# x read in 32-wide blocks and turned by VectorE, in another order of work: two graph attention layers in float32 on one Trainium2 core

## The chip, the cores and the metric

The kernel runs on one core of a Trainium2 chip. Its engines are named as in the profile: PE is TensorE (PEld its weight loads), DVE is VectorE, ACT is ScalarE, POOL is GpSimd, SP is SyncE, which here only issues DMAs. The metric is the time on the device in microseconds, lower is better.

## What is computed

128 graphs, each with 128 nodes of 384 features. Two layers follow each other; each is an attention over 12 heads of width 32 in which the adjacency matrix is added to the scores, then a residual and a layer norm.

```python
# x: (128, 128, 384), adj: (128, 128, 128)
def L0(x, adj):                        # scale = 384 ** -0.5
    q, k, v = x @ Wq.T, x @ Wk.T, x @ Wv.T + bv        # split into 12 heads
    scores = einsum('bqhd,bkhd->bhqk', q, k) * scale + 2 * adj
    p = softmax(where(any(scores != 0), scores, -inf)) # a row of zeros gives 0
    return einsum('bhqk,bkhd->bqhd', p, v) @ Wo.T + bo
def L1(x, adj):                        # scale = 32 ** -0.5
    q, k, v = x @ Wq + bq, x @ Wk + bk, x @ Wv + bv
    scores = einsum(q, k) * scale + beta * adj
    return einsum(softmax(where(adj > 0, scores, -9e15)), v)
x = layernorm(x + L0(x, adj))
x = layernorm(x + L1(x, adj))
```

## The kernel before

**Pairs and stages.** The graphs are worked on two at a time, in 64 pairs. One run of each engine's `body` is an iteration n; it does different stages of different pairs: `n` is the pair whose layer 0 scores are made now, `p1` the next one, `m1` to `m5` are one to five pairs back. In a name such as `attend(1, m3, 0, r)` the first number is the layer, then come the pair and the graph of the pair. Iterations -1 to 7 and the last ones are written out; 54 between them run in a loop of two iterations a turn. Each engine's `body` is a hand-written list, and an engine works through it strictly in that order. The engines meet only through semaphores.

**Products.** A projection is a float32 product made of three faster ones: both factors are split into a high part and a rest (`_hi`, `_lo`), and `split_product` (L363) adds hi*hi, lo*hi and hi*lo over three chunks of 128 features: nine matmuls. They are 256 columns wide for q and k (`project_qk`, six a layer and pair) and 384 for v and the output (`project_v`, `project_out0`).

**x before the first projection.** SP loads a graph of x to `x_in` (node on the partition, `load_x`). PE transposes it in three blocks (`transpose_x`, L348), ACT takes the high part from PSUM (`high_xT`, L514), DVE the rest (`low_xT`, L714). POOL adds the output bias to `x_in` and keeps it as `x_bo` for the residual (L873).

**Layer 0's softmax.** `scores` (PE, L416) writes four banks. `negate` (DVE, L692) adds the adjacency, negates, and finds the row minimum. ACT makes the exps (L589). `fold_scores0` (POOL, L896 and L899) adds the negated scores in halves, and `abs_max` (DVE, L741) finishes that, to know rows of zeros; `inverse_sums0` (DVE, L776, L780) gives the factor and `normalise0` (POOL, L914, three pieces) applies it. `flip_probs` (DVE, L708) transposes each 32 by 32 block of the probabilities into `flip0`, and `spread_probs` (SP, L300) moves the blocks to their places in `prob0T` by four DMAs of 192 KB. `attend` (PE, L432) uses them. `flip0` is also where the fold writes, so `fold_scores0` waits until the spread of the graph before has landed. Layer 1 does the same without the fold, through `stage` and `prob1T`.

**PSUM.** Eight banks: four for scores, four as a ring for all else; the list `RING_USERS` deals the ring's banks out in turn, and a PE block first waits for the last reader of its bank.

**Narrow blocks.** Scores use 32 rows of the array and attention 32 columns at a time, in 12 matmuls each, and transposes are plain float32 matmuls against the identity. All other blocks are the projections' 128 by 128 products.

Of the kernel before, what the change touches and what calls it, by code (L numbers as in the profile page):

```python
# [31 lines left out]
NB = N // HD  # L32
PAIRS = NG // 2
# [9 lines left out]
FIRST, LAST = -1, PAIRS + 4  # L43
# [10 lines left out]
RING_USERS = ["pv0_0", "pv1_0", "g1_0", "ot_0", "v1_0", "wo_0", "v0_1", "xt0",  # L54
              "xt1", "g1_1", "pv1_1", "v1_1", "ot_1", "g1_2", "pv0_1", "g0_0",
              "g0_1", "g1_3", "wo_1", "g1_4", "g1_5", "g0_2", "x1t0", "g0_3",
              "g0_4", "g0_5", "x1t1", "v0_0"]
RING = 4
assert len(RING_USERS) % RING == 0
# [52 lines left out]
def build(nc, x, adj, wts, bv0, bo0, bq1, bk1, bv1, beta, out):  # L112

    with ExitStack() as ctx:
# [26 lines left out]
        x_in = [sb(f"x_in{b}", [P, 2, D]) for b in range(2)]  # L141
# [9 lines left out]

        xT_hi, xT_lo = sb("xT_hi", [P, C, G2], F32R), sb("xT_lo", [P, C, G2], F32R)
# [33 lines left out]
        x_loaded, adj0_loaded, adj1_loaded = sems("x_loaded"), sems("adj0_loaded"), sem("adj1_loaded")  # L186
# [8 lines left out]
        xt_done, x1t_done = sem("xt_done"), sem("x1t_done")  # L195
# [34 lines left out]
        def _(sp):  # L230
            def load_x(q):
                if q.valid():
                    b = q.parity

                    sp.wait_ge(xt_done, q.plus(-2).count(1, 1, 1))
                    sp.wait_ge(x_bo_done, q.plus(-2).count(1, 1, 1))
                    for g in range(2):
                        sp.dma_start(x_in[b][:, g, :], x[bass.ds(2 * q.index() + g, 1)].rearrange("g (j a) d -> a j (g d)", j=NB)
                                     ).then_inc(x_loaded[b], 16)
# [41 lines left out]
            load_weights(WV0)  # L281
# [21 lines left out]
            def body(r, off):  # L303
# [3 lines left out]
                spread_probs(1, m4, 1)  # L307
                keep_x1(m3)
                if not is_peeled(r, off, -1):
                    load_adj0(p1)  # L310
                spread_probs(0, m1, 1)
                store(m5, 1)
                spread_probs(1, m3, 0)
                load_adj1(m1)
                spread_probs(0, n, 0)
                load_x(p2)
                store(m4, 0)
# [8 lines left out]
        def _(pe):  # L326

            read = [(xt_lo_done, 0, 0, 0, 0)] * 4
# [132 lines left out]
            def body(r, off):  # L461
# [5 lines left out]
                transpose_out1(m4, 0, r)  # L467
                project_v(1, m2, 0, r)
                project_out0(m1, 0, r)
                project_v(0, n, 1, r)  # L470
                scores(1, m3, 1, r)
                transpose_x(p1, 0, r)
                transpose_x(p1, 1, r)
                project_qk(1, m2, 1, r)
                attend(1, m4, 1, r)
                project_v(1, m2, 1, r)
                transpose_out1(m4, 1, r)
                project_qk(1, m2, 2, r)
# [492 lines left out]
```

## Time and profile before

| | us |
|---|---|
| median of 3 runs | 2143.37 (2141.89 to 2144.39) |
| the profiled execution | 2141.5 |
| its span, first to last instruction | 2139.7 |
| PE busy in the span | 2061.3 |
| DVE, ACT, POOL busy | 1870.9, 1834.0, 1511.2 |

The span is what the trace covers; the time of an execution has 1.8 us around it. A busy time counts overlapping instructions of an engine once. PE is pipelined: a row of it lasts until its result is out, so rows overlap, and how long PE is held is read from one start to the next. SP's rows show the issue of DMAs, not their transfer.

### The profile page before, as it was taken

How to read it: one execution, taken by the hardware profiler on the slowest of the kernel's cores; microseconds unless marked ns; L12 is line 12 of the kernel's file. 1: busy time of each engine (PE TensorE's matmuls, PEld its weight loads, DVE VectorE, ACT ScalarE, POOL GpSimd, SP SyncE). 2: the span in 40 equal slices, each digit the busy share in tenths (PEclk: the TensorE clock that was granted, in tenths of full speed). 3: DMA queues.
4: the chain of work that ended last, by engine and by line, in shares of the span. 5: the costliest groups of instructions: out<-in, count | busy, mean ns of one | idle time of the engine just before them, and what ended most of it. 6: DMA issues, size and time to landing. Idle time of an engine off the chain costs nothing.

```text
span 2139.7 us, 86405 instructions
## 1 busy us (share of the span) xinstructions
PE 2061.3 (96%) x23808; PEld 1924.5 (90%) x23808; DVE 1870.9 (87%) x8452; ACT 1834.0 (86%) x7688; POOL 1511.2 (71%) x2059
## 2 busy tenths in 40 slices
PE   5799999999999999999999999999999999999984
PEld 4799999999999999999999999999999999999873
DVE  4588989999999999999999999999999899999875
ACT  4489888889889889889889889888988988988875
POOL 3667777777777777777777777777777777777663
PEclk9999999999999999999999999999999999999997
DMA  4255665665565565565565565556556556556454
GB/s 133 60 131 132 149 160 126 147 157 131 146 155 132 145 155 134 145 150 136 143 150 139 144 146 142 141 146 148 135 146 152 131 146 155 131 144 158 119 136 119
DMA packets 234654, 299.36 MB, mean 140 GB/s; under 512 B 26704, under 2 KB 226384, under 8 KB 234576
## 3 DMA queue, kind: packets, MB, share of 16 engines
q1 hardware_dynamic: 234576, 298.43, 56.5%
q8 instruction: 36, 0.59, 0.1%
q14 instruction: 42, 0.34, 0.0%
HBM read 46.67 MB, written 25.17 MB: 34 GB/s over the span
## 4 chain that ended last, share of the span: by engine, by line
PE 86%; POOL 5%; issue 3%; DMA 3%; DVE 2%; SPq 2%; ACT 0%; POOLq 0%; DVEq 0%
PE r_bank L365 22%; PE r_bank L366 20%; PE r_bank L367 20%; PE s_bank L416 10%; PE r_bank L432 8%; PE r_bank L348 2%; DMA prob0T<-flip 2%; PE r_bank L358 2%; PE r_bank L444 2%; POOL prob L914 2%; SPq L300 1%; POOL flip L896 1%; DVE flip L708 1%; DMA prob1T<-stage 0%; POOL norm L857 0%
## 5 line engine op out<-in xcount | busy, mean ns | idle before, releaser
L589 ACT ACTIVATE prob<-neg_s,heads 128x128 f32<-128x128 f32 x3072 | 1190.1, 393 | 49.5 <-DVE flip L708 42.5
L589 ACT ACTIVATION_READ_ACCUMULATOR prob<-neg_s,heads 128x1 f32 x3072 | 592.1, 193 | 0.0
L896 POOL TENSOR_TENSOR flip<-neg_s 128x768 f32<-128x768 f32 x128 | 235.7, 1842 | 265.3 <-DMA prob0T<-flip 255.1
L914 POOL TENSOR_TENSOR prob<-prob,heads 128x512 f32<-128x512 f32 x384 | 388.8, 1040 | 19.2 <-DVE heads L780 15.5
L365 PE MATMUL r_bank<-xT_hi,w_hi 128*128 128x256 f32 x1152 | 344.6, 299 | 16.6 <-DVE xT_lo L714 10.9
L692 DVE CUSTOM_DVE_ANT_0 neg_s<-s_bank,bias 128x128 f32<-128x128 f32 x1536 | 333.9, 286 | 15.4 <-PE s_bank L416 14.3
L365 PE MATMUL r_bank<-x1T_hi,w_hi 128*128 128x256 f32 x1152 | 342.3, 297 | 3.3 <-DVE x1T_lo L714 1.8
L692 DVE CUSTOM_DVE_ANT_0 neg_s<-s_bank,adj 128x128 f32<-128x128 f32 x1536 | 334.0, 286 | 1.7 <-PE s_bank L416 0.5
L366 PE MATMUL r_bank<-xT_lo,w_hi 128*128 128x256 f32 x1152 | 326.0, 283 | 0.0
L367 PE MATMUL r_bank<-xT_hi,w_lo 128*128 128x256 f32 x1152 | 325.9, 283 | 0.0
L367 PE MATMUL r_bank<-x1T_hi,w_lo 128*128 128x256 f32 x1152 | 323.9, 281 | 0.0
L366 PE MATMUL r_bank<-x1T_lo,w_hi 128*128 128x256 f32 x1152 | 323.8, 281 | 0.0
L692 DVE DVE_READ_ACCUMULATOR2_ANT heads<- 128x1 f32 x3072 | 256.1, 83 | 0.1
L708 DVE STREAM_TRANSPOSE flip<-prob 128x1536 f32<-128x1536 f32 x128 | 227.7, 1779 | 24.3 <-POOL prob L914 18.9
L365 PEld LDWEIGHTS r_bank<-xT_hi,w_hi 128*128 128x128 f32 x1152 | 218.2, 189 | 32.6 <-DVE xT_lo L714 11.4
L365 PEld LDWEIGHTS r_bank<-x1T_hi,w_hi 128*128 128x128 f32 x1152 | 217.2, 189 | 12.4 <-DVE x1T_lo L714 2.0
L708 DVE STREAM_TRANSPOSE stage<-prob 128x1536 f32<-128x1536 f32 x128 | 224.0, 1750 | 3.8 <-DMA prob1T<-stage 3.8
L366 PEld LDWEIGHTS r_bank<-xT_lo,w_hi 128*128 128x128 f32 x1152 | 219.0, 190 | 0.0
L367 PEld LDWEIGHTS r_bank<-xT_hi,w_lo 128*128 128x128 f32 x1152 | 218.4, 190 | 0.0
L366 PEld LDWEIGHTS r_bank<-x1T_lo,w_hi 128*128 128x128 f32 x1152 | 217.7, 189 | 0.0
L367 PEld LDWEIGHTS r_bank<-x1T_hi,w_lo 128*128 128x128 f32 x1152 | 217.0, 188 | 0.0
L854 POOL TENSOR_SCALAR norm<-norm 128x1 f32<-128x1 f32 x256 | 56.7, 221 | 177.1 <-DVE norm L673 161.6
(83 smaller groups left out, 5443.9 us busy)
## 6 DMA issues: line engine op xcount, KB each, us to landing
prob0T<-flip SPq DMA_DIRECT2D x512, 192.0 KB, 3.6
prob1T<-stage SPq DMA_DIRECT2D x512, 192.0 KB, 3.6
x_in<-in_x_dram SPq DMA_DIRECT2D x128, 192.0 KB, 3.2
x_late<-x SPq DMA_DIRECT2D x64, 384.0 KB, 4.3
out_dram<-y SPq DMA_DIRECT2D x128, 192.0 KB, 2.7
adj<-in_adj_dram SPq DMA_DIRECT2D x256, 64.0 KB, 2.9
prob<-in_L_gnn_Wq_dram SPq DMA_DIRECT2D x1, 576.0 KB, 5.7
prob0T<-in_L_gnn_Wk_dram SPq DMA_DIRECT2D x1, 576.0 KB, 6.6
```

Source lines behind the costliest of these rows:

```text
L348: mm = pe.transpose(ring(f"xt{g}")[:, c * P:(c + 1) * P], x_in[q.parity][:, g, c * P:(c + 1) * P], ident[:])
L365: pe.matmul(dst, a_hi(c), b_hi(c), start=(c == 0), stop=False)
L366: pe.matmul(dst, a_hi(c), b_lo(c), start=False, stop=False)
L367: mm = pe.matmul(dst, a_lo(c), b_hi(c), start=False, stop=(c == C - 1))
L416: mm = pe.matmul(s_bank[j][:, c * N:(c + 1) * N], qT[layer][q.parity][rows, c, m], kT[layer][q.parity][rows, c, m], start=True, stop=True)
L432: mm = pe.matmul(ring(name)[HD * j:HD * (j + 1), c * N:(c + 1) * N], v[layer][q.parity][:, g, f], probT[layer][:, :, HC * c + j, :], start ...
L589: act.activation(prob[layer][:, h, :], neg_s[layer][:, h, :], ACT.Exp, bias=neg_max[layer][:, h:h + 1], scale=-1.0, accum_out=row_sum[laye ...
L692: dve.tensor_tensor_reduce(neg_s[layer][:, h, :], s_bank[b][:, (h // HC) * N:(h // HC + 1) * N], (adj0, bias1)[layer][q.parity][:, g, :], ...
L708: dve.transpose(flip[layer].rearrange("p (j h b) -> p h j b", j=NB, h=H), prob[layer][:].rearrange("p h (j a) -> p h j a", j=NB)).then_inc ...
L854: pool.tensor_scalar(var_eps[layer][g][:], mean_var[layer][g][:, 1:2], EPS, None, ALU.add).then_inc(rstd_steps[layer], 1)
L896: pool.tensor_tensor(fold_a, neg_s[0][:, :, 0:N // 2], neg_s[0][:, :, N // 2:N], ALU.add).then_inc(fold_steps, 1)
L914: pool.tensor_tensor(prob[0][:, hs, :], prob[0][:, hs, :], inv_sum0[:, hs].unsqueeze(2).to_broadcast([P, HC, N]), ALU.mult).then_inc(probn ...
```

## The change

Where x is turned: SP now loads x a second time, as `x_q`. Four DMAs a pair (`load_q`) put the 96-feature column block i of both graphs on partitions 32i to 32i+31, with the row block of 32 nodes along the free dimension. One 32 by 32 block transpose of DVE a graph (`flip_x`) then gives `xT` in SBUF, with the features in another order of rows; the rows of the three layer 0 weights are loaded in that same order (`load_rows`, four DMAs each, two of the weights from ACT's queue). `transpose_x` and its two places in the ring are gone. ACT takes the high part from `xT`, POOL the rest (`low_xT`, before on DVE). `x_bo` is loaded directly and POOL adds the bias in place.

The order of all five lists is another one, and so is `RING_USERS`. The second graph's values are projected one iteration earlier, and there is one more written-out iteration at the start.

```diff
-FIRST, LAST = -1, PAIRS + 4
+FIRST, LAST = -2, PAIRS + 4
...
+            def load_q(q):
+                if q.valid():
+                    sp.wait_ge(xflip_done, q.count(1, 0, 0))
+                    for i in range(NB):
+                        sp.dma_start(x_q[HD * i:HD * (i + 1), :, :],
+                                     x[bass.ds(2 * q.index(), 2)].rearrange("g (j a) d -> a (g j) d", j=NB)[:, :, QD * i:QD * (i + 1)]
+                                     ).then_inc(xq_loaded, 16)
...
-            load_x(Pair(0, 0))
-            load_weights(WQ0)
-            load_weights(WK0)
+            load_q(Pair(0, 0))
+            load_rows(WV0)
...
-            def transpose_x(q, g, r):
-                if q.valid():
-                    pe.wait_ge(*last_read(read, BANK[f"xt{g}"], r))
-                    read[BANK[f"xt{g}"]] = (xt_lo_done, q.off, 1, g, 1)
-                    pe.wait_ge(x_loaded[q.parity], q.loads(2))
-                    for c in range(C):
-                        mm = pe.transpose(ring(f"xt{g}")[:, c * P:(c + 1) * P],
-                                          x_in[q.parity][:, g, c * P:(c + 1) * P], ident[:])
-                    mm.then_inc(xt_done, 1)
...
+            def flip_x(q, g):
+                if q.valid():
+                    dve.wait_ge(xq_loaded, q.count(8 * NB, 1, 8 * NB))
+                    dve.wait_ge(xt_lo_done, q.plus(-1).count(1, g, 1))
+                    dve.transpose(xT[:, :, g * N:(g + 1) * N].rearrange("p c (j a) -> p c j a", j=NB),
+                                  x_q[:, g * NB:(g + 1) * NB, :].rearrange("p j (c b) -> p c j b", c=C)
+                                  ).then_inc(xflip_done, 1)
...
+            def low_xT(q, g):
+                if q.valid():
+                    pool.wait_ge(xt_hi_done, q.count(1, g, 1))
+                    if g == 0:
+                        pool.wait_ge(v_done[0], q.count(1, 0, 0))
+                        pool.wait_ge(g_done[0], q.count(3, 0, 0))
+                    m = slice(g * N, (g + 1) * N)
+                    pool.tensor_tensor(*(t.rearrange("p c (a j) -> p c a j", j=NB) if i != 1 else t.rearrange("p c (j a) -> p c a j", j=NB)
+                                        for i, t in enumerate((xT_lo[:, :, m], xT[:, :, m], xT_hi[:, :, m].bitcast(F32)))), ALU.subtract
+                                      ).then_inc(xt_lo_done, 1)
```

On PE, in the middle of an iteration, before: layer 1's scores are followed by the transposes of x, and its attention stands alone between projections.

```order
L416 MATMUL s_bank<-k1T,q1T 128x128 x12
L348 MATMUL r_bank<-ident,x_in 128x128 x6
L365 MATMUL r_bank<-x1T_hi,w_hi 128x256
L366 MATMUL r_bank<-x1T_lo,w_hi 128x256
L367 MATMUL r_bank<-x1T_hi,w_lo 128x256
...
L432 MATMUL r_bank<-prob1T,v_0 32x128 x12
L365 MATMUL r_bank<-w_hi,x1T_hi 128x384
```

The same place now: the transposes of x are gone, and the attention of layer 0's first graph, that of layer 1's second and the scores of layer 1 stand next to each other.

```order
L368 MATMUL r_bank<-w_hi,x1T_lo 128x384
L433 MATMUL r_bank<-prob0T,v_0 32x128 x12
L433 MATMUL r_bank<-prob1T,v_1 32x128 x12
L417 MATMUL s_bank<-k1T,q1T 128x128 x12
L366 MATMUL r_bank<-w_hi,o0T_hi 128x384
```

Over a whole iteration the runs of narrow blocks (scores, attentions, transposes that touch each other) go from nine to six.

On POOL, from `normalise0` of the second graph to the next fold, before:

```order
L914 TENSOR_TENSOR prob<-prob,heads 128x512 x3
L884 TENSOR_SCALAR mask<-adj 128x128
L886 TENSOR_SCALAR adj<-adj,beta_col 128x128
L889 TENSOR_TENSOR bias_1<-adj,mask 128x128
...
L906 TENSOR_TENSOR y_0<-y_0,x_late 128x384
L873 TENSOR_TENSOR x_bo<-x_in,bo_row 128x384 x2
L896 TENSOR_TENSOR flip<-neg_s 128x768
```

and now, from the last step of the first bias on:

```order
L897 TENSOR_TENSOR bias_0<-adj,mask 128x128
L906 TENSOR_TENSOR xT_lo<-xT,xT_hi 128x3x128
L892 TENSOR_SCALAR mask<-adj 128x128
L894 TENSOR_SCALAR adj<-adj,beta_col 128x128
L897 TENSOR_TENSOR bias_0<-adj,mask 128x128
L863 TENSOR_SCALAR norm_0<-norm_0 128x1
L866 TENSOR_TENSOR norm_0<-norm_0,neg_half 128x1
L870 TENSOR_SCALAR norm_0<-norm_0 128x1
L906 TENSOR_TENSOR xT_lo<-xT,xT_hi 128x3x128
L915 TENSOR_TENSOR flip<-neg_s 128x768
```

The residuals of both layers moved behind the fold; both `low_xT` and one `inverse_std` stand ahead of it.

On SP, the DMAs around the border of two iterations, before:

```order
L300 DMA prob0T<-flip 128x1x384 x4
...
L238 DMA x_in<-in_x_dram 128x1x384
...
L259 DMA out_dram<-y_0 32x4x384
L300 DMA prob1T<-stage 128x1x384 x4
...
L269 DMA x_late<-x_0 128x768
...
L246 DMA adj_0<-in_adj_dram 128x1x128
...
L300 DMA prob0T<-flip 128x1x384 x4
```

and now:

```order
L309 DMA prob1T<-stage 128x1x384 x4
...
L236 DMA x_q<-in_x_dram 32x8x96
...
L275 DMA x_late<-x_0 128x768
...
L309 DMA prob0T<-flip 128x1x384 x4
```

The four issues of `x_q` (one is shown) stand between those of `prob1T` and those of `prob0T`. The loads of `x_bo` and both adjacency loads are now ahead of these `prob1T`.

## Rows read from the trace of the kernel before

**Rows 1.** The page: busy time, share of the span, instructions of each engine

```profile
PE 2061.3 (96%) x23808; PEld 1924.5 (90%) x23808; DVE 1870.9 (87%) x8452; ACT 1834.0 (86%) x7688; POOL 1511.2 (71%) x2059
```

**Rows 2.** Busy time by stretch: length, PE, PEld, DVE, ACT, POOL, clock, DMA share, GB/s

```profile
130.00:2045.00 1915.00, 1912.33 (x22296) 1791.14 (x22292) 1740.74 (x7910) 1705.07 (x7189) 1403.84 (x1914) 1.00 0.58 143
```

**Rows 3.** Timeline of PE: start, length, line, out<-in, count

```profile
98.56 0.95 PE L416 MATMUL s_bank<-k0T,q0T 32*128 32x128 f32 x24
...
1007.35 0.86 PE L432 MATMUL r_bank<-prob0T,v 128*32 128x128 f32 x24
1008.03 0.84 PE L432 MATMUL r_bank<-prob1T,v 128*32 128x128 f32 x24
...
1016.87 0.88 PE L348 MATMUL r_bank<-ident,x_in 128*128 128x128 f32 x6
1017.51 0.37 PE L365 MATMUL r_bank<-x1T_hi,w_hi 128*128 128x256 f32 x1
1017.71 0.28 PE L366 MATMUL r_bank<-x1T_lo,w_hi 128*128 128x256 f32 x1
1017.83 0.28 PE L367 MATMUL r_bank<-x1T_hi,w_lo 128*128 128x256 f32 x1
...
1018.75 0.86 PE L432 MATMUL r_bank<-prob1T,v 128*32 128x128 f32 x24
1019.54 0.44 PE L365 MATMUL r_bank<-w_hi,x1T_hi 128*128 128x384 f32 x1
...
2045.54 0.95 PE L416 MATMUL s_bank<-k0T,q0T 32*128 32x128 f32 x24
```

**Rows 4.** Timelines of POOL, DVE and SP: the ring from fold to fold

```profile
1021.08 1.85 POOL L896 TENSOR_TENSOR flip<-neg_s 128x768 f32<-128x768 f32 x1 [1.22 <-DMA prob0T<-flip]
...
1024.04 0.55 DVE L741 TENSOR_REDUCE heads<-flip 128x12 f32<-128x384 f32 x1 [0.43 <-POOL flip L899]
...
1025.41 3.04 POOL L914 TENSOR_TENSOR prob<-prob,heads 128x512 f32<-128x512 f32 x3
...
1028.57 1.78 DVE L708 STREAM_TRANSPOSE flip<-prob 128x1536 f32<-128x1536 f32 x1 [0.27 <-POOL prob L914]
...
1030.38 3.02 SPq L300 DMA_DIRECT2D prob0T<-flip  x4
...
1036.73 1.84 POOL L896 TENSOR_TENSOR flip<-neg_s 128x768 f32<-128x768 f32 x1 [2.58 <-DMA prob0T<-flip]
```

**Rows 5.** The same timelines, in the turn before

```profile
1004.87 1.84 POOL L896 TENSOR_TENSOR flip<-neg_s 128x768 f32<-128x768 f32 x1 [2.26 <-DMA prob0T<-flip]
...
1008.14 0.54 DVE L741 TENSOR_REDUCE heads<-flip 128x12 f32<-128x384 f32 x1
...
1013.04 1.69 SPq L246 DMA_DIRECT2D adj<-in_adj_dram  x2
1014.83 3.05 SPq L300 DMA_DIRECT2D prob0T<-flip  x4
```

**Rows 6.** Waits of the whole span: total us, times, longest

```profile
POOL flip L896 <- DMA prob0T<-flip: 255.1, 127, 8.3
...
DVE heads L741 <- POOL flip L899: 43.5, 71, 4.4
```

**Rows 7.** Timeline of POOL: from the first make_bias1 to what follows the second

```profile
1012.70 0.66 POOL L884 TENSOR_SCALAR mask<-adj 128x128 f32<-128x128 f32 x1
...
1016.91 1.01 POOL L906 TENSOR_TENSOR y<-y,x_late 128x384 f32<-128x384 f32 x1
```

**Rows 8.** Groups by shape (busy us, mean ns), and the page's DMA queue

```profile
L714 DVE TENSOR_TENSOR xT_lo<-r_bank,xT_hi 128x384 fp32r<-128x384 f32 x128 | 63.1, 532 | 6.9 <-ACT xT_hi L514 4.1 <-issue 2.8
...
q1 hardware_dynamic: 234576, 298.43, 56.5%
```

**Rows 9.** Timelines of PE and POOL at the start

```profile
15.74 0.55 PE L365 MATMUL r_bank<-xT_hi,w_hi 128*128 128x256 f32 x1 [9.71 <-DVE xT_lo L714]
...
16.17 0.25 POOL L939 TENSOR_SCALAR bq1s<-bqk 128x3 f32<-128x3 f32 x1 [14.51 <-DMA bqk<-in_L_gnn_bk_dram]
```

More of the change, by code:

```diff
@@ L32 @@
 NB = N // HD
+QD = D // NB
 PAIRS = NG // 2
@@ L139, in build @@
         neg_half = sb("neg_half", [P, 1])
-        x_in = [sb(f"x_in{b}", [P, 2, D]) for b in range(2)]
+        x_q = sb("x_q", [P, 2 * NB, QD])
         x_bo = [sb(f"x_bo{b}", [P, 2, D]) for b in range(2)]
@@ L313, in body @@
                 spread_probs(1, m3, 0)
+                spread_probs(0, n, 0)
+                store(m4, 0)
                 load_adj1(m1)
-                spread_probs(0, n, 0)
-                load_x(p2)
-                store(m4, 0)
+                load_x(p1)
+                if not is_peeled(r, off, -1):
+                    load_adj0(p1)
+                spread_probs(1, m3, 1)
             iterations(sp, body)
@@ L326, in _ @@
         def _(pe):
-            read = [(xt_lo_done, 0, 0, 0, 0)] * 4
+            read = [(v_out[0], 0, 0, 0, 0)] * 4
             s_read = [(neg_done[0], 0, 0, 0, 0)] * HC
@@ L502, in _, with load_rows, rows_xT @@
         def _(act):
+            def load_rows(i):
+                for k in range(NB):
+                    act.dma_start(w_stage[i][HD * k:HD * (k + 1), :, :],
+                                  wts[i][QD * k:QD * (k + 1), :].rearrange("(c b) o -> b c o", c=C)).then_inc(w_loaded[i], 16)
+            load_rows(WQ0)
+            load_rows(WK0)
             def high_weights(*which):
                 for i in which:
-                    act.wait_ge(w_loaded[i], 16)
+                    act.wait_ge(w_loaded[i], 16 * (NB if i in (WV0, WQ0, WK0) else 1))
                     act.activation(w_hi[i][:], w_stage[i], ACT.Copy).then_inc(w_hi_done[i], 1)
+            def rows_xT(g):
+                return xT[:, :, g * N:(g + 1) * N].rearrange("p c (j a) -> p c a j", j=NB)
             def high_xT(q, g):
                 if q.valid():
-                    act.wait_ge(xt_done, q.count(1, g, 1))
+                    act.wait_ge(xflip_done, q.count(1, g, 1))
                     if g == 0:
@@ L513, in high_xT @@
                         act.wait_ge(g_done[0], q.count(3, 0, 0))
[L514 to L516 removed]
+                    act.activation(xT_hi[:, :, g * N:(g + 1) * N].rearrange("p c (a j) -> p c a j", j=NB), rows_xT(g), ACT.Copy).then_inc(xt_hi_done, 1)
             def high_x1T(q, g):
@@ L595, in body @@
                 n = Pair(r, off)
-                m5, m4, m3, m2, m1, p1 = (n.plus(-5), n.plus(-4), n.plus(-3), n.plus(-2), n.plus(-1), n.plus(1))
-                high_o0T(m1, 0)
-                exps(1, m3, 0, 2, 4)
-                out1T_out(m4, 0)
-                exps(1, m3, 0, 4, 8)
-                qk_out(1, m2, 0, r)
-                exps(1, m3, 0, 8, 12)
-                norm_apply1(m5, 1)
-                exps(0, n, 0, 0, 6)
-                high_xT(p1, 0)
+                m4, m3, m2, m1, p1 = (n.plus(-4), n.plus(-3), n.plus(-2), n.plus(-1), n.plus(1))
+                exps(1, m3, 0, 0, 6)
+                high_xT(p1, 0)
+                exps(1, m3, 0, 6, 10)
+                qk_out(1, m2, 0, r)
+                qk_out(1, m2, 1, r)
+                high_o0T(m1, 0)
+                exps(1, m3, 0, 10, 12)
                 high_xT(p1, 1)
@@ L870, in residual0 @@
                     pool.wait_ge(x_loaded[b], q.loads(2))
-                    pool.wait_ge(y0_done, q.plus(-2).count(1, 1, 1))
                     for g in range(2):
-                        pool.tensor_tensor(x_bo[b][:, g, :], x_in[b][:, g, :], bo_row[:], ALU.add
+                        pool.tensor_tensor(x_bo[b][:, g, :], x_bo[b][:, g, :], bo_row[:], ALU.add
                                            ).then_inc(x_bo_done, 1)
@@ L919, in body @@
                 n = Pair(r, off)
-                m4, m2, m1 = (n.plus(-4), n.plus(-2), n.plus(-1))
+                m4, m3, m2, m1, p1 = (n.plus(-4), n.plus(-3), n.plus(-2), n.plus(-1), n.plus(1))
                 normalise0(m1, 1)
                 make_bias1(m2, 0)
+                low_xT(p1, 0)
                 make_bias1(m2, 1)
-                residual1(m4, 0)
-                residual0(n, r)
+                inverse_std(1, m4, 0)
+                low_xT(p1, 1)
                 fold_scores0(n, 0)
@@ L930, in body @@
                 residual1(m4, 1)
-                inverse_std(1, m4, 0)
+                residual0(n, r)
+                inverse_std(1, m4, 1)
                 inverse_std(0, m1, 1)
                 fold_scores0(n, 1)
-                inverse_std(1, m4, 1)
+                residual1(m3, 0)
                 if is_peeled(r, off, 0):
```

132 lines of the change are left out of this document (62 added, 70 removed).

## The prediction

> **What bounds the kernel now.** I read the page's busy line, then two stretches by engine, then the tensor engine's timeline, then the waits, and last I followed the one loop of dependences that the waits point to.
>
> Busy shares leave little room: PE 96%, DVE 87%, ACT 86% [rows 1]. Between 130 and 2045 us PE is busy 1912.33 of 1915 us at a granted clock of 1.00, that is the 2.4 GHz level, against 1741 us of DVE, 1705 of ACT and 1404 of POOL [rows 2]. What comes after 2045 is the drain. The scores of layer 0's second graph start at 98.56 us for pair 2 and at 2045.54 us for pair 63 [rows 3]: 61 pairs in 1946.98 us, **31.92 us a pair**. So PE sets the pace, and what is taken from it is won, until something else comes due.
>
> That something is visible. POOL's fold waits for the landing of `prob0T` 127 times, 255 us in all [rows 6]. The fold writes `flip0`, the very buffer that the turned probabilities of the graph before leave by DMA. So there is a **ring**: fold, abs_max and inverse (DVE), normalise0 (POOL), flip (DVE), four DMAs issued by SP, landing, next fold. It runs once a graph, twice a pair. One turn of it starts at 1021.08 and ends at 1036.73: 15.65 us, made of 2.96 (fold, until DVE takes over at 1024.04), 1.37 to the start of normalise0, 3.04 of that, 0.12, a 1.78 transpose, 0.03, and 6.35 from SP's first issue to the next fold [rows 4]. Nothing in it stands idle. The other turn of a pair must take 31.92 - 15.65 = 16.27 us. The one from 1004.87 shows what it has to spare: its fold of 2.96 us would be over at 1007.8 and DVE comes at 1008.14; its transpose, in the same rhythm, ends at about 1014.5 and SP comes at 1014.83, after other loads [rows 5]. That is 0.3 twice. The ring alone therefore needs about 15.65 + 15.7 = **31.35 us a pair**, only 0.57 under today's pace. In 71 of 128 folds DVE already stood waiting for POOL [rows 6], which says the same.
>
> **The change, part by part.**
>
> *PE loses work.* The six transposes of x take 1016.87 to 1017.51, 0.64 us a pair [rows 3]. The order also joins narrow blocks. Two neighbouring attentions start 0.68 apart (1007.35, 1008.03), one alone holds PE for 0.79 (1018.75 to 1019.54), and the projection's first matmul behind a narrow block is followed 0.20 later (1017.51 to 1017.71) where 0.12 is the rhythm (1017.71 to 1017.83; the rows are longer and overlap) [rows 3]. So a run of narrow blocks pays about 0.1 on its way in and as much on its way out. Before, a pair has nine such runs (of transposes, scores, attentions), after it six. Three fewer at somewhat under 0.1 a side come to about 0.23. PE's need falls to 31.92 - 0.64 - 0.23 = **31.05 us**.
>
> *DVE is even.* It drops two `xT_lo` subtractions of 532 ns [rows 8] and gains two transposes 384 wide. A transpose 1536 wide takes 1.78 [rows 4]; a quarter of that is 0.44, and at most it keeps a fixed part of some 0.2, 0.6. Two of them cost -0.2 to +0.15 us a pair. I take 0. DVE is busy 1741/60 = 29.0 us a pair and stays below both other bounds.
>
> *ACT is even.* `high_xT` reads SBUF instead of PSUM, same width; nothing between -0.1 and +0.4 a pair reaches the path with 28.4 busy of 31.
>
> *POOL takes over `low_xT`*, two subtractions 384 wide, both in the stretch between normalise0 of one turn and the fold of the next. Nearest row: 1.01 us for a plain add of that width [rows 7]. The stretch is from 1028.45 (1025.41 + 3.04) to 1036.73: 8.28 us [rows 4]. In it now stand two `make_bias1`, 4.21 us (1012.70 to 1016.91) [rows 7], one `inverse_std` (it fits in the 1.4 between fold and normalise0 [rows 4]) and the two subtractions, 2.0, with 0.1 of gaps: 7.7 us. Spare: 0.6. So each may cost 1.3 before the fold is late. `low_xT` reads `xT` in steps of 128 bytes, which no row shows; I bound it by 1.0 and 2.0 and take 1.0 to 1.3.
>
> The Trainium skill (GPSIMD Engine Reference, § 7 Performance pitfalls for Q7 kernels) says that a read whose step is over 8 bytes costs a GpSimd kernel half as much again. No run here shows it. By that estimate, 1.5 each, the fold would be 0.4 late.
>
> *SP issues four more DMAs a pair*, `x_q`, 29 instead of 25. Four of `prob0T` hold it for 3.02 us [rows 4], 0.76 each, so SP is busy some 22 us of 31. The order matters: from the issue for the first graph's probabilities, 15 DMAs (4 `prob0T`, the store, 2 `adj1`, 2 `x_bo`, 2 `adj0`, 4 `prob1T`), then the four `x_q`, then `keep_x1`, and only then the second turn's `prob0T`. That is 15 x 0.76 + 4q + 0.6 = 12.0 + 4q, and it must be over within the ring's 15.7. It is, with q up to 0.93. With q = 0.76 there are 0.7 us to spare. Bounds for q: 0.76 from that row, and twice that, 1.5, since one has 256 pieces where one of `prob0T` has 128; less than 0.76 would change nothing. I take 0.76, as the time of an issue is not seen to follow its size: four `prob0T` of 192 KB take 3.05, two loads of `adj`, 64 KB each, 1.69 [rows 5].
>
> *DMA engines.* The hardware queue's 234576 packets fill 56.5% of 16 engines [rows 8], 0.082 us each. `x_q` adds 1024 a pair, 65536: at the same time each +15.7 points, at half of it +8. The share goes to 65 to 72%. Landings in the ring may lengthen: 0 to 0.3 a turn; `x_q` is in flight just ahead of one turn in two. I take 0.1 a pair.
>
> *The start is longer.* PE's projections begin at 15.74, on `xT_lo` from DVE; POOL's first real step waits until 16.17 for the last small load [rows 9]. Now `xT_lo` is POOL's, behind that load, and three more DMAs are issued ahead of it (17 instead of 14): 16.2 + 3 x 0.76 = 18.5, plus two `low_xT` of 1.0 to 1.4, so PE begins at 20.5 to 21.3, some 5.2 later. Also the second graph's values are projected ahead of the first scores: nine matmuls 384 wide at 1.5 times the 0.12 of a 256 wide one [rows 3], 1.6 us. The scores, and with them the ring, start **6.8 us** later (4 to 8). Nothing hides this: from there on the ring decides.
>
> *The drain* keeps its chain (last scores, exps, flip, spread, attend, layer norm, store): 0, within 2 us.
>
> **The sum.** PE would allow 31.05, the ring 31.35, DVE less; with 0.1 for landings and jitter now that nothing else absorbs them, 31.45 us a pair. 60 pairs x (31.92 - 31.45) = 28.2 us won, 6.8 lost: the span goes from 2139.7 to 2118.3. The profiled execution took 2141.5, 1.8 over its span, and the median of the runs shown is 1.9 above that: **2122.0 us**. With 31.3 to 31.7 a pair and a start of 4 to 8 us it is 2110 to 2138.
>
> **The rivals.**
>
> *PE keeps the pace.* The ring's turns may shrink, as SP and DVE now come to them in another order, and landings vary. Then a pair takes PE's 31.05 to 31.15: 60 x 0.82 = 49 less, 6.8 more, 2101 us. For it: PE is the busiest engine on every view. Against: no link of the turn in [rows 4] is touched by the change.
>
> *The gain is swallowed on POOL.* With `low_xT` at 1.5 each, by the row's width and a cost half as large again, the fold is 0.4 late in one turn a pair: 31.85, 60 x 0.07 = 4 won, 6.8 lost, 2146 us, the same as before. This is the time that the rule of the GPSIMD Engine Reference in the Trainium skill gives. [...]
>
> *SP is late, the kernel slower.* If one `x_q` takes SP q over 0.93, the second turn's `prob0T` issue waits and each turn of that kind grows by 4(q - 0.93). At q = 1.2 that is 1.1 us a pair: 31.45 + 1.1 = 32.55, 60 x 0.63 = 38 more, plus 6.8: 2188 us. By over 0.2% slower it is from q = 1.04. For it: twice the pieces in each DMA. Against: the even pace named above.
>
> **How the numbers follow.** Chances: forecast 0.50, PE's pace 0.22, swallowed on POOL 0.12, SP late 0.12, the rest, mostly a longer start, 0.04. The time is the forecast's, 2122. The range leaves out the slow rival and the fastest edge: 2101 to 2143. About 0.2%, 4.3 us, is what a measurement of this kernel can tell. Faster than 2139.1: the forecast, PE's pace and a part of the swallowed case, 0.76. Same: 0.11. Slower: 0.13.
>
> **What would show it.** The fold on POOL should still wait for `prob0T`, and now PE should show small idle times, 0.2 to 0.4 a pair, in front of transposes or first attentions. If PE is gapless the second case holds. A `low_xT` row above 1.3 and folds that start without waiting show the third; SP's first `prob0T` issue coming more than 0.1 behind its transpose in one turn of two shows the fourth. The first projection should start near 20 us. I am wrong altogether if the narrow blocks do not save PE anything, or if attentions placed early wait for probabilities.

## The result: slower, 2157.3 us, with PE no longer the bound

The changed kernel takes 2157.29 us (median of 4 runs, 2155.69 to 2157.82) beside 2143.08 for the kernel before on the same chip: a ratio of 1.0065, 95% interval 1.0053 to 1.0077. The forecast was 2122 us, with a range of 2101 to 2143. The profiled execution's span went from 2139.7 to 2153.9 us, 14.2 more. The forecast was faster, and the time moved the other way. The page of the changed kernel, busy time of each engine (before: [rows 1]):

```profile
PE 2011.7 (93%) x23424; PEld 1871.0 (87%) x23424; DVE 1872.6 (87%) x8452; ACT 1871.8 (87%) x7688; POOL 1662.0 (77%) x2187
```

PE is 50 us less busy, as intended, and the kernel is longer. Its stretch in the middle by engine (length, PE, PEld, DVE, ACT, POOL, clock, DMA share, GB/s; before: [rows 2]):

```profile
600.00:1600.00 1000.00, 973.53 (x11505) 908.20 (x11506) 912.96 (x4151) 911.18 (x3764) 809.21 (x1063) 1.00 0.63 157
```

PE now stands idle 26.5 us of 1000, at a granted clock of 1.00 as before, that is at 2.4 GHz. I take the length of a pair from the first `normalise0` of pair 8 and of pair 60: 31.91 us before, 31.89 after. PE is busy 0.9735 x 31.89 = 31.05 us of a pair, the number of the prediction to the hundredth; only the time does not follow it. (A busy time is a rough measure of a need, since short waits can hide in overlapping rows: the runs below with this same list on PE give 31.04 to 31.31.) The waits of the whole span (total us, times, longest) say who holds it (before: [rows 6]):

```profile
POOL flip L915 <- DMA prob0T<-flip: 191.6, 125, 6.1
...
ACT prob L597 <- DVE flip L716: 80.6, 64, 3.4
DVE heads L750 <- POOL flip L918: 61.9, 102, 8.2
PE r_bank L433 <- DVE v L778: 58.4, 61, 12.2
...
POOL prob L933 <- DVE heads L789: 42.9, 65, 1.9
```

The fold still waits for the spread 125 times, DVE waits for the fold in 102 turns instead of 71, and PE waits once a pair, at its first attention, for values that DVE has not yet taken out. The page's chain of work that ended last was PE's before and no longer is (shares of the span, before and after):

```profile
PE 86%; POOL 5%; issue 3%; DMA 3%; DVE 2%; SPq 2%; ACT 0%; POOLq 0%; DVEq 0%
...
POOL 39%; issue 30%; DVE 11%; PE 10%; DMA 4%; SPq 2%; POOLq 2%; DVEq 1%; ACT 0%; ACTq 0%
```

Two turns of the ring, one pair, on the timelines of POOL, DVE and SP (before: [rows 4] and [rows 5]):

```profile
1032.65 1.84 POOL L915 TENSOR_TENSOR flip<-neg_s 128x768 f32<-128x768 f32 x1 [0.24 <-DMA prob0T<-flip]
...
1036.97 3.04 POOL L933 TENSOR_TENSOR prob<-prob,heads 128x512 f32<-128x512 f32 x3
...
1040.13 1.78 DVE L716 STREAM_TRANSPOSE flip<-prob 128x1536 f32<-128x1536 f32 x1 [0.23 <-POOL prob L933]
...
1041.94 3.02 SPq L309 DMA_DIRECT2D prob0T<-flip  x4
1045.18 0.62 SPq L265 DMA_DIRECT2D out_dram<-y  x1
...
1048.45 1.85 POOL L915 TENSOR_TENSOR flip<-neg_s 128x768 f32<-128x768 f32 x1 [2.25 <-DMA prob0T<-flip]
...
1051.43 0.55 DVE L750 TENSOR_REDUCE heads<-flip 128x12 f32<-128x384 f32 x1
...
1053.12 3.04 POOL L933 TENSOR_TENSOR prob<-prob,heads 128x512 f32<-128x512 f32 x3 [0.51 <-DVE heads L789]
...
1055.94 0.55 DVE L778 TENSOR_TENSOR v<-r_bank,bv_row 128x384 f32<-128x384 f32 x1
1056.41 1.77 DVE L716 STREAM_TRANSPOSE flip<-prob 128x1536 f32<-128x1536 f32 x1
...
1056.41 0.53 SPq L275 DMA_DIRECT2D x_late<-x  x1
1058.21 3.02 SPq L309 DMA_DIRECT2D prob0T<-flip  x4
...
1064.57 1.84 POOL L915 TENSOR_TENSOR flip<-neg_s 128x768 f32<-128x768 f32 x1 [0.39 <-DMA prob0T<-flip]
```

15.80 and 16.12 us: 31.92. SP's first issue comes 0.03 behind each transpose, so SP is not late; POOL is through with its other work 0.24 and 0.39 us before each of the folds that follow `low_xT`, so POOL is not late either. I measured every link over turns 10 to 117, 54 of each graph (means, us; "g0" is the turn that starts with the first graph's fold; "landing" is from the issue of the fourth DMA until it has landed):

| link | before g0 | before g1 | after g0 | after g1 |
|---|---|---|---|---|
| fold on POOL | 2.92 | 2.94 | 2.92 | 2.93 |
| until abs_max starts | 0.03 | **0.27** | 0.03 | 0.03 |
| abs_max to the factor | 1.22 | 1.46 | 1.22 | 1.52 |
| gap, normalise0 | 3.20 | 3.13 | 3.18 | 3.12 |
| gap, flip | 1.90 | 1.90 | 1.90 | **1.98** |
| until SP issues | 0.03 | **0.23** | 0.03 | 0.03 |
| first to fourth issue | 2.02 | 2.04 | 1.98 | 2.04 |
| landing of the fourth | 4.18 | 4.32 | **4.51** | **4.38** |
| landing to next fold | 0.08 | 0.07 | 0.08 | 0.07 |
| turn | 15.57 | 16.35 | 15.83 | 16.10 |

Before, only 0.23 + 0.21 = 0.44 us of a pair were slack (the bold entries of "before g1", less the 0.03 that these links take at least), so the ring needed 31.47. After, that slack is gone and the links that carry load grew by 0.33 (landing g0), 0.06 (landing g1), 0.06 (factor) and 0.08 (the values that DVE takes between `negate` and the flip, seen at 1055.94), together 0.53; three others shrank by 0.07 in all. The ring's pace is 31.93, and the kernel's. It is a coincidence of sizes that this is also what PE needed before.

Where the 14.2 us came in, by the first `normalise0` of a pair, after minus before:

| pair 0 | pair 8 | pair 20 | pair 60 | pair 63 | end of span |
|---|---|---|---|---|---|
| +8.24 | +11.73 | +12.63 | +10.82 | +13.52 | +14.19 |

So the start costs 8.2, the first eight pairs 3.5, the long middle gives back 0.9, the last three pairs cost 2.7, and the drain 0.7. Timelines of POOL and PE at the start: the first scores of the kernel before, then the changed kernel (before: [rows 9]):

```profile
25.68 0.95 PE L416 MATMUL s_bank<-k0T,q0T 32*128 32x128 f32 x24
...
17.13 0.25 POOL L960 TENSOR_SCALAR bq1s<-bqk 128x3 f32<-128x3 f32 x1 [15.47 <-DMA bqk<-in_L_gnn_bk_dram]
18.23 2.32 POOL L906 TENSOR_TENSOR xT_lo<-xT,xT_hi 128x384 fp32r<-128x384 f32 x2 [0.84 <-ACT xT_hi L524]
...
20.81 0.55 PE L366 MATMUL r_bank<-xT_hi,w_hi 128*128 128x256 f32 x1 [20.81 <-POOL xT_lo L906]
...
32.69 0.95 PE L417 MATMUL s_bank<-k0T,q0T 32*128 32x128 f32 x24
...
35.59 2.32 POOL L906 TENSOR_TENSOR xT_lo<-xT,xT_hi 128x384 fp32r<-128x384 f32 x2 [15.04 <-ACT xT_hi L524]
37.88 1.82 POOL L915 TENSOR_TENSOR flip<-neg_s 128x768 f32<-128x768 f32 x1
```

PE begins at 20.81 (forecast 20.5 to 21.3) and the first scores come 7.0 us later than before (forecast 6.8). Then the first fold finds both `low_xT` of pair 1 ahead of it on POOL, and the ring starts 8.2 late. The groups of the changed kernel by shape (busy us, mean ns) and its DMA queue price the new operations (before: [rows 8]):

```profile
L906 POOL TENSOR_TENSOR xT_lo<-xT,xT_hi 128x384 fp32r<-128x384 f32 x128 | 156.3, 1222 | 15.9 <-ACT xT_hi L524 15.9
L524 ACT ACTIVATE xT_hi<-xT 128x384 fp32r<-128x384 f32 x128 | 115.2, 901 | 2.1 <-DVE xT L729 2.1
L729 DVE STREAM_TRANSPOSE xT<-x_q 128x384 f32<-128x384 f32 x128 | 71.9, 563 | 5.6 <-DMA x_q<-in_x_dram 5.6
...
q1 hardware_dynamic: 303456, 322.43, 60.3%
```

### The profile page after: what moved, and what is told of

The parts are those of the page before. It is cut to its first block, busy times and chain, and to the rows that moved or that the text cites. A ratio compares the mean times of both kernels' runs of the same rounds, so it can differ in the third digit from the quotient of the medians.

```text
span 2153.9 us, 86362 instructions
## 1 busy us (share of the span) xinstructions
PE 2011.7 (93%) x23424; PEld 1871.0 (87%) x23424; DVE 1872.6 (87%) x8452; ACT 1871.8 (87%) x7688; POOL 1662.0 (77%) x2187
## 3 DMA queue, kind: packets, MB, share of 16 engines
q1 hardware_dynamic: 303456, 322.43, 60.3%
## 4 chain that ended last, share of the span: by engine, by line
POOL 39%; issue 30%; DVE 11%; PE 10%; DMA 4%; SPq 2%; POOLq 2%; DVEq 1%; ACT 0%; ACTq 0%
POOL prob L933 11%; POOL flip L915 9%; POOL norm L866 4%; DMA prob0T<-flip 4%; DVE flip L716 4%; POOL adj L894 3%; POOL xT_lo L906 3%; POOL mask L892 3%; PE r_bank L366 3%; PE r_bank L368 2%; PE r_bank L367 2%; DVE norm L678 2%; SPq L309 2%; DVE neg_s L700 2%; POOL norm L863 2%
## 5 line engine op out<-in xcount | busy, mean ns | idle before, releaser
L366 PE MATMUL r_bank<-x1T_hi,w_hi 128*128 128x256 f32 x1152 | 332.6, 289 | 5.0 <-DVE x1T_lo L722 5.0
L716 DVE STREAM_TRANSPOSE flip<-prob 128x1536 f32<-128x1536 f32 x128 | 227.0, 1773 | 21.4 <-POOL prob L933 21.3
L906 POOL TENSOR_TENSOR xT_lo<-xT,xT_hi 128x384 fp32r<-128x384 f32 x128 | 156.3, 1222 | 15.9 <-ACT xT_hi L524 15.9
```

Source lines behind the costliest of these rows:

```text
L366: pe.matmul(dst, a_hi(c), b_hi(c), start=(c == 0), stop=False)
L716: dve.transpose(flip[layer].rearrange("p (j h b) -> p h j b", j=NB, h=H), prob[layer][:].rearrange("p h (j a) -> p h j a", j=NB)).then_inc ...
L906: pool.tensor_tensor(*(t.rearrange("p c (a j) -> p c a j", j=NB) if i != 1 else t.rearrange("p c (j a) -> p c a j", j=NB) for i, t in enum ...
```

## The experiments

My theory: the ring through `flip0` sets the pace, and the changed order made it longer, above all by what SP issues behind the first graph's `prob0T`. Rivals: the traffic of `x_q` slows the landings; or the order has another bound of its own; or the new path of x costs what it saves. "Pair" below is the mean of pairs 8 to 60. Each kernel was timed beside the one before on the same chip, and its ratio is to that time, which was 2142.3 to 2143.6 us.

| kernel | median us | ratio to before, 95% | pair | PE busy in 600:1600 |
|---|---|---|---|---|
| before | 2143.08 | | 31.91 | 1000.00 |
| after | 2157.29 | 1.0065 (1.0053 to 1.0077) | 31.89 | 973.53 |
| own_after | 2130.75 | 0.9939 (0.9923 to 0.9954) | 31.67 | 980.12 |
| own_before | 2131.42 | 0.9940 (0.9925 to 0.9956) | 31.89 | 1000.00 |
| sp_order | 2148.72 | 1.0025 (1.0016 to 1.0034) | 31.74 | 978.44 |
| store_first | 2147.61 | 1.0028 (1.0019 to 1.0038) | 31.70 | 979.56 |
| xq_once | 2157.91 | 1.0060 (1.0046 to 1.0074) | 31.92 | 973.18 |
| low_plain | 2158.57, one run | | 31.92 | 974.21 |
| own_after_v | 2127.03 | 0.9934 (0.9917 to 0.9951) | 31.64 | 989.67 |
| best1 | 2117.33 | 0.9876 (0.9860 to 0.9893) | 31.52 | 988.80 |
| x_only | 2436.38 | 1.1374 (1.1355 to 1.1393) | 36.64 | 956.24 |
| x_only_own | 2382.39 | 1.1114 (1.1096 to 1.1133) | 35.94 | 954.72 |
| x_only2 | 2139.42 | 0.9982 (0.9973 to 0.9992) | 31.68 | 993.71 |
| x_only2_own | 2109.67 | 0.9844 (0.9827 to 0.9860) | 31.38 | 999.51 |

### Is it the ring? Cut it in both kernels

The fold writes a free part of `stage` instead of `flip0`, and so needs no landing. The same edit in both kernels:

```diff
-        fold_a = flip0[:, 0:H * N // 2].rearrange("p (h k) -> p h k", h=H)
-        fold_b = flip0[:, H * N // 2:H * N * 3 // 4].rearrange("p (h k) -> p h k", h=H)
+        fold_a = stage[:, H * N:H * N * 3 // 2].rearrange("p (h k) -> p h k", h=H)
+        fold_b = fold_a[:, :, 0:N // 4]
...
-                    pool.wait_ge(probT_loaded[0], q.count(16 * NB, g, 0))
```

> The changed kernel, but the fold of layer 0 writes to a free part of `stage` instead of to `flip0`, so it no longer waits for the spread of the graph before to land. Theory R (ring: fold, abs_max, normalise0, flip, spread, landing, fold sets the pace of 31.9 us a pair now): the ring is cut, a pair falls to about PE's 31.05 to 31.3, 60 pairs x 0.7 = 40 us less, some 2115 us. Rival E (the engines' new orders collide elsewhere, DVE and ACT waits; the ring only looks tight): a pair stays at 31.7 to 31.9, within 10 us of 2157.

> The kernel before with the same cut of the ring. Theory R says that PE, not the ring, set the pace before (PE busy 1912 of 1915 us): the middle stays at 31.9 us a pair, and only the first pairs, where PE is not full, get shorter: 5 to 25 us less, 2118 to 2138. If the ring had set the pace before as well, a pair would get shorter in the middle too.

The changed kernel falls by 26.5 us, the kernel before by 12. In the kernel before nothing changes in the middle (31.89, PE 1000.00 of 1000): it wins while the pipeline fills, where PE is not yet full and the ring decides, 258 us for the first eight pairs before and 248 with the cut. In the changed kernel 14 of its gain lie in those pairs too (261 and 247), and the rest in the middle. So the ring was the bound in the changed kernel, shown. But the 40 us that I expected did not come: a pair falls only to 31.67, far from PE's 31.05, so there is a second bound close below. The waits of own_after between 600 and 1600 us:

```profile
PE r_bank L433 <- DVE v L778: 14.8, 31, 0.5
```

### What lengthened the landing?

sp_order: both `adj` loads and the store are issued ahead of the first graph's `prob0T`, only `load_x` behind.

```diff
-                spread_probs(0, n, 0)
-                store(m4, 0)
                 load_adj1(m1)
-                load_x(p1)
                 if not is_peeled(r, off, -1):
                     load_adj0(p1)
+                store(m4, 0)
+                spread_probs(0, n, 0)
+                load_x(p1)
```

> The changed kernel with another order on SP only: both adjacency loads and the store of m4 are issued ahead of layer 0's first spread of the iteration instead of right behind it. Theory S (the store and the loads that start right behind the spread lengthen the landing of its fourth DMA, 4.18 us before, 4.51 now): it falls back to about 4.2, a pair gets 0.3 shorter, 18 us less, 2139 us. Theory X (the added traffic of x_q does it): no change, 2157 within 4.

store_first: the store alone is moved ahead, the loads stay behind.

```diff
+                store(m4, 0)
                 spread_probs(0, n, 0)
-                store(m4, 0)
                 load_adj1(m1)
```

> The changed kernel with one move alone: SP issues the store of layer 1's rows ahead of the DMAs of prob0T for the first graph, so that it is no longer the DMA right behind them; the loads of adj1 and x_bo stay behind. My theory: it is the write to device memory right behind that makes the landing of the fourth DMA 0.3 us longer: 4.51 falls to 4.2, that turn of the ring from 15.83 to 15.55, and the time by 60 x 0.25 = 15 us at most, less what the order's other loops hold: 2142 to 2152 us. Rival: any DMA 3 us behind does it, loads too: the landing stays at 4.4 to 4.5 and the time at 2155 to 2158 us.

xq_once: `x_q` is loaded for pair 0 only, so all layer 0 projections use pair 0's rows of x, and 252 DMAs are left out.

```diff
             def load_q(q):
-                if q.valid():
+                if is_peeled(q.r, q.off, 0):
...
-                    dve.wait_ge(xq_loaded, q.count(8 * NB, 1, 8 * NB))
+                    dve.wait_ge(xq_loaded, 16 * NB)
```

> The changed kernel, but x_q is loaded for pair 0 only and all pairs turn that x: four DMAs a pair, 1024 small packets, are left out (the result is that of other inputs). Theory X (traffic and issues of x_q lengthen the ring): the landings fall back to 4.2, 0.3 to 0.4 a pair less, 2135 us. Theory S: landings stay, 2155 to 2158 us.

Landing of the fourth DMA and length of the turns, means over the same turns:

| | landing g0 | landing g1 | turn g0 | turn g1 |
|---|---|---|---|---|
| after | 4.51 | 4.38 | 15.83 | 16.10 |
| sp_order | 4.19 | 4.39 | 15.57 | 16.18 |
| store_first | 4.01 | 4.37 | 15.37 | 16.34 |
| xq_once | 4.49 | 4.42 | 15.83 | 16.11 |
| x_only2 (below) | 3.94 | 4.37 | 15.32 | 16.37 |

One first-graph turn of store_first on the timelines of SP and POOL, with two loads where the changed kernel has the store:

```profile
1006.44 3.02 SPq L309 DMA_DIRECT2D prob0T<-flip  x4
1009.76 1.41 SPq L259 DMA_DIRECT2D adj<-in_adj_dram  x2
...
1012.43 1.83 POOL L915 TENSOR_TENSOR flip<-neg_s 128x768 f32<-128x768 f32 x1 [1.71 <-DMA prob0T<-flip]
```

The store is the cause: without it right behind, two loads of `adj` (64 KB each) in its place, the landing is 0.50 shorter, more than I had claimed. Loads behind do less: in x_only2, further below, nothing at all is issued for 3.9 us behind the fourth DMA, and it lands after 3.94; the two loads of `adj` make it 4.01, and two loads of x (192 KB each), in sp_order and in the kernel before, 4.19 and 4.18. So in the kernel before the store was not next: a load of x was, and the store came 4.45 us behind the fourth DMA, when that had landed. `x_q` does nothing. The store is behind the second graph's DMAs in every kernel here, and that landing is 4.3 to 4.4 everywhere. What the store does to the DMA ahead of it, these runs don't show. The time followed only in part: sp_order won 9 of the 18 us expected of it, store_first 10 of at most 15. In store_first the ring got 0.46 shorter in one turn and the pair only 0.19: turn g1 grew from 16.10 to 16.34, since `abs_max` now comes 0.18 behind the fold and the factor takes 1.63 instead of 1.52. There DVE is late; I take it for the second bound that own_after met, which no run here isolates.

### The price of `low_xT`

low_plain reads `xT` without its 128-byte steps, so `xT_lo` pairs values that don't belong together.

```diff
-                    pool.tensor_tensor(*(t.rearrange("p c (a j) -> p c a j", j=NB) if i != 1 else t.rearrange("p c (j a) -> p c a j", j=NB)
+                    pool.tensor_tensor(*(t
```

> The changed kernel, but low_xT on POOL reads and writes its three operands in plain order instead of reading xT in steps of 128 bytes (the rests then stand in the wrong places). If the step costs, low_xT falls from 1222 ns to the 1010 of a plain subtraction; if POOL shares a port with DVE at that place and the step is free, it stays at 1200. In either case the ring has no part in it, and the time stays at 2157 within 5.

Its group:

```profile
L906 POOL TENSOR_TENSOR xT_lo<-xT,xT_hi 128x384 fp32r<-128x384 f32 x128 | 129.4, 1012 | 16.4 <-ACT xT_hi L524 16.4
```

1012 ns plain, 1222 with the step: 21% more, inside the 1.0 to 1.3 that I took. The Trainium skill (GPSIMD Engine Reference, § 7 Performance pitfalls for Q7 kernels) gives half as much again for such a step; for this subtraction of two inputs, one of them with the step, the measurement decides, 21%. And the kernel is no faster for it (2158.57, a single run), so the rival on POOL falls.

### The bounds behind the ring

own_after_v: own_after, and DVE takes the second graph's values out ahead of the long `negate`.

```diff
-                negate(0, n, 0, (0, 1, 2, 3))
                 values_out(0, n, 1)
+                negate(0, n, 0, (0, 1, 2, 3))
```

> The changed kernel with the ring cut (fold in `stage`), and on DVE the second graph's values, values_out(0, n, 1), taken out of PSUM ahead of negate(0, n, 0) instead of behind it. With the cut alone a pair takes a steady 31.67 us with PE idle 0.5 in front of the first attention. Theory V: that is a second loop, PE's scores (1, m2, 0), DVE's negates, values_out, the bank that the attention needs; moved ahead, the wait goes and a pair comes to PE's 31.05 to 31.2: 60 x 0.5 = 30 us less, some 2101 us. Rival D: DVE as a whole (busy 29.1 and many short waits) is what takes 31.67; then nothing or at most 5 us is won.

PE's wait at the first attention is gone, but a pair takes 31.64 instead of 31.67, where I had expected at most 31.2 and 2101 us. The next loop stood right behind. One pair of own_after_v, timelines of PE, its weight loads, DVE and POOL:

```profile
994.97 0.95 PE L417 MATMUL s_bank<-k1T,q1T 32*128 32x128 f32 x24
...
996.10 0.29 DVE L700 CUSTOM_DVE_ANT_0 neg_s<-s_bank,bias 128x128 f32<-128x128 f32 x1 [0.88 <-PE s_bank L417]
...
999.57 0.54 DVE L750 TENSOR_REDUCE heads<-stage 128x12 f32<-128x384 f32 x1
...
1001.28 3.04 POOL L932 TENSOR_TENSOR prob<-prob,heads 128x512 f32<-128x512 f32 x3 [0.55 <-DVE heads L789]
...
1011.17 1.24 POOL L906 TENSOR_TENSOR xT_lo<-xT,xT_hi 128x384 fp32r<-128x384 f32 x1
...
1012.46 0.19 PEld L366 LDWEIGHTS r_bank<-xT_hi,w_hi 128*128 128x128 f32 x1 [0.43 <-POOL xT_lo L906]
...
1026.62 0.95 PE L417 MATMUL s_bank<-k1T,q1T 32*128 32x128 f32 x24
```

From layer 1's scores (994.97) DVE negates, then finds the zero rows of the second graph (999.57); POOL normalises it, makes both biases, a layer norm's factor and the second `low_xT` (done at 1012.41); PE starts the next pair's projection at once (1012.46), after a wait, and comes to the same scores of the next pair at 1026.62: 31.65 us, in which POOL, PE and DVE each had to wait for the step before. This loop exists only because `low_xT` now is POOL's and stands behind `normalise0`; before, PE's transposes and DVE fed that projection.

best1: own_after_v, with the second `low_xT` directly behind the first.

```diff
                 low_xT(p1, 0)
+                low_xT(p1, 1)
                 make_bias1(m2, 1)
                 inverse_std(1, m4, 0)
-                low_xT(p1, 1)
```

> The changed kernel with the fold and the turned probabilities in buffers of their own, values_out ahead of negate, and both low_xT ahead of the second make_bias1 and of inverse_std on POOL. My theory: once the ring is cut, what holds a pair at 31.65 us is the loop from layer 1's scores over negate, normalise0 and low_xT back to the projection; with low_xT 3 us earlier PE's wait for it goes, and PE's own need is the bound: 31.1 to 31.3 us a pair, 2098 to 2110 us, and PE busy over 98% of its middle. Rival: the loops of the order lie close together, the next one (the bias or the layer norm's factor, now later) holds 31.5 or more, 2118 us or more.

9.7 us faster than own_after_v, and the wait for `xT_lo` has left the middle, so that loop was a bound. But a pair still takes 31.52, and I had expected 31.1 to 31.3 and at most 2110 us, so the rival came nearer. Waits of PE between 600 and 1600 us in best1:

```profile
PE r_bank L359 <- ACT x L576: 5.0, 32, 0.2
PE r_bank L433 <- DMA prob1T<-stage: 4.4, 15, 0.5
```

These are 9 of its 11 idle us; half of them are now at an attention of layer 1, which waits for the landing of its own probabilities. Which loop lies behind that I did not settle.

### The new path of x without the new order

These four keep the lists of the kernel before and add only the new path of x; where its steps stand is my choice (`residual0` moves behind the first `normalise0` with it). x_only puts each `low_xT` ahead of a `make_bias1`, both `flip_x` together, `load_q` behind the first spread; x_only_own adds the cut.

```diff
                 normalise0(m1, 1)
+                low_xT(p1, 0)
                 make_bias1(m2, 0)
+                low_xT(p1, 1)
                 make_bias1(m2, 1)
```

> The kernel before in its own order, with only the new way of x: x_q, flip_x on DVE where low_xT stood, low_xT on POOL ahead of both make_bias1, residual0 behind normalise0; x_q is loaded one pair earlier. No transposes on PE, so PE needs 31.92 - 0.64 = 31.28 us a pair. Theory R: the ring, with the store behind the second turn only, needs 31.47, so 60 x 0.4 = 24 less, 5 more at the start: 2124 us. If the new order of work and not the ring's length were what kept the changed kernel at 31.93, it would be PE's pace: 2110 us. If the way of x itself costs (POOL late with the fold), 2143 or more.

> The same with the fold in `stage`: the ring cut. Theory R: PE's pace, 31.28 us a pair, and shorter first pairs: 2131 (the kernel before with the cut) + 5 - 60 x 0.6 = 2100 us. Rival: as in the changed kernel, another loop holds at 31.6 or more: 2120 us.

Both are over a tenth slower, and both theories missed, for a reason that the waits of x_only name:

```profile
POOL xT_lo L906 <- ACT xT_hi L524: 354.8, 64, 15.4
DVE xT L729 <- POOL xT_lo L906: 234.4, 124, 3.7
```

ACT makes `xT_hi` late in its list, where it stood when PE made the transposes. `low_xT` early on POOL waits 5.5 us a pair for it, with the biases and the fold queued behind. PE then stands idle 44 us between 600 and 1600, and its granted clock there is 0.93 (0.96 in x_only_own) where every other kernel here has 1.00; what the clock adds was not separated. This tells of my placement, not of the path. So x_only2 moves `low_xT` just ahead of the fold, where ACT is through, spreads the two `flip_x`, and loads `x_q` ahead of the first spread:

```diff
                 spread_probs(1, m3, 0)
                 load_adj1(m1)
+                if not is_peeled(r, off, -2):
+                    load_q(p2)
                 spread_probs(0, n, 0)
-                load_x(p2)
                 store(m4, 0)
+                load_x(p1)
...
                 inverse_sums1(m3, 1)
+                flip_x(p2, 0)
                 norm_input0(m1, 1)
                 flip_probs(1, m3, 1)
                 low_x1T(m1, 0)
                 negate(1, m2, 0, (0, 1, 2, 3))
+                flip_x(p2, 1)
...
                 residual1(m4, 0)
-                residual0(n, r)
+                low_xT(p1, 0)
+                low_xT(p1, 1)
                 fold_scores0(n, 0)
```

> The kernel before, its order kept, with the new path of x alone: x_q loaded ahead of the first graph's prob0T issues, flip_x placed behind inverse_sums1 of the second graph and behind negate of layer 1, low_xT on POOL just ahead of the first fold. The ring of the kernel before stays. My theory: the ring's 31.47 us a pair, measured as the sum of its links, decides: 31.45 to 31.6, 2120 to 2130 us, and the order of the changed kernel, not its path of x, is what lost the gain. Rival: low_xT or the four issues more on SP lengthen the ring also here: 31.9 or more, 2143 us or more.

> The same with the fold in a buffer of its own, so the ring is cut. My theory: PE's need without the transposes, 31.92 - 0.64 = 31.28, decides: 31.3 to 31.4 us a pair, 2098 to 2115 us. Rival: a loop through low_xT or flip_x, as in the changed kernel with the same cut, holds 31.65 or more: 2125 us or more.

With the ring, the path of x wins 0.2% (0.9982): 31.68 a pair, 0.1 above what I expected, and 2139 us instead of 2120 to 2130. It is not the ring's links alone that hold it: in its second turn `abs_max` comes 0.49 us behind the fold, so DVE is late there as in store_first. With the ring cut it takes 2109.67 us, the fastest kernel here, 1.6% under the one before. Its middle (columns as above):

```profile
600.00:1600.00 1000.00, 999.51 (x11666) 932.91 (x11666) 911.55 (x4200) 929.14 (x3827) 821.84 (x1086) 1.00 0.64 158
```

PE is full again, at 31.38 a pair. The cut alone gave 12, the path of x alone 3, both together 33: each had been hiding the other's gain.

## Why the prediction was wrong, point by point

- **PE's need, 31.05: borne out by its busy time** (31.05), though no run with this order had PE full at that pace. The parts are less sure. x_only2_own loses the transposes and keeps the old order, and its PE is busy 0.9995 x 31.38 = 31.37, so by busy times they gave 0.55, not 0.64, and the joined narrow blocks with the rest of the order 0.32, not 0.23. Busy times of one and the same list differ by up to 0.27 between runs, so these differences of 0.09 show nothing.
- **The ring as the next bound: right for the ring as it came out.** own_after against own_before shows it. Close below stood a bound that the prediction had not seen.
- **"The ring alone therefore needs about 15.65 + 15.7 = 31.35": mis-sized.** The slack in the second turn, "0.3 twice", was read from one pair; over 54 pairs it is 0.23 + 0.21, and the ring needed 31.47. That is 0.12 a pair, 7 us.
- **"I take 0.1 a pair" for landings and jitter: the first step that failed.** The measured growth of the links is 0.46 (31.93 - 31.47), 0.33 of it one landing. I looked for the cause in the new `x_q`, "in flight just ahead of one turn in two", which costs nothing (xq_once). What mattered stood in the order that I had printed and priced only as SP's time: the store, next behind the first graph's spread (store_first: 0.50). My own bound of 0 to 0.3 a turn held the 0.06 of one turn and nearly the 0.33 of the other; the sum took a value near its lower end, and the range stopped at 31.7 a pair.
- **"No link of the turn is touched by the change": wrong.** DVE's neighbours in the second turn changed: 0.06 on the way to the factor, 0.08 ahead of the flip.
- **DVE "stays below both other bounds": wrong as a reading, and the second step that failed.** A busy share does not show the loops that an engine takes part in. With the ring cut, the loop over `negate`, `normalise0` and `low_xT` held 31.65, and even a shorter ring (store_first, sp_order) gave only 31.70 to 31.74. So the forecast of 31.45 was out of reach for this order even with the landing that I assumed: with no ring at all it takes 31.67 (own_after).
- **POOL: right.** 1222 ns, the fold late by nothing, on average 0.45 us of spare (0.10 to 1.25 over the turns) where I had 0.6.
- **SP: right, and cheaper.** Four `x_q` are issued in 2.1 us on average (1.90 in the pair shown), about 0.5 each where I took 0.76, and in that pair SP is through 1.3 us before the second turn's spread is due (1056.94 against 1058.21). The slow rival was slow for another reason than the kernel is.
- **DMA share: below the range.** 60.3% against 65 to 72: the new packets took less time each than the mean of the old ones.
- **ACT: mis-sized, with no effect seen.** `high_xT` went from 488 to 901 ns, 0.8 us a pair where I allowed 0.4.
- **Start: 6.8 right for the scores** (7.0), partly by luck: the last small load came at 17.13 and not at 18.5, but then `low_xT` waited for ACT until 18.23. It was short by 1.2 for the ring, since two `low_xT` stand ahead of the first fold. And the first eight pairs add 3.5: there the kernel before already ran at the ring's pace with PE not full, so a longer ring costs from the first turn; the first graph's landings alone are 3.0 longer over these pairs. PE's granted clock between 54 and 108 us is 0.78 of the 2.4 GHz level where it was 0.91, with PE busy 34 us there where it was 43. But every turn of the ring from 74.6 us on is made up of its own links alone, and own_after, with 0.87, takes 247 us for these pairs; so I put the loss down to the ring and not to the clock.
- **Drain: right** (0.7). The last three pairs cost 2.7 that I had at nothing. The trace shows one piece: at 2012.31, early in the first iteration behind the loop, DVE stands idle 2.53 us with no wait that the profile shows. In the changed order that falls ahead of the values and the flip of the ring, and this turn takes 18.75 us; its like before took 16.66. The rest is open.

By size: the middle was to bring 28.2 and brought 0.9, a miss of 27; start and first pairs 4.9; the end 3.4. Together 35.6, the distance from -21.4 to +14.2.

## What to carry to other kernels

When a loop of dependences lies close under the busiest engine (here 31.47 beside 31.91 us, 1.4%), taking work from that engine can win no more than that distance until the loop is cut, and a new order can lose it all. Measure each link over all turns, since slack read from one pair was a third too large, and ask of every edit what it does to each link. Behind the first loop look for the next one. Cutting a false dependence (here a scratch buffer shared with a DMA's source) may show nothing by itself in the middle and still be worth more than the change planned on top. A DMA order is not only issue time: see what lands, or stores, right behind the transfer that someone waits for.

## What the runs showed of the hardware

- The fourth of four DMAs of 192 KB from SBUF to SBUF lands 4.51 us after its issue with a store of 192 KB to device memory issued right behind it (after), 4.01 with two loads of 64 KB there instead (store_first), 4.19 with two loads of 192 KB (sp_order), 3.94 with nothing for 3.9 us (x_only2); means of 54 turns.
- The issue of a DMA of 256 pieces of 384 bytes holds SP about 0.5 us (four in 2.1 on average), less than one of `prob0T` (four in 3.1).
- The same copy on ACT, 384 wide, takes 488 ns from PSUM in the old layout and 901 ns from SBUF with its source read in steps. Which of the two differences makes it so was not separated.
